# A graph network's node update: the last tile's product made while edges are counted, and six half groups instead of ten between a layer's steps

## The reference

```python
x_norm = layer_norm(x, norm_g, norm_b)
out1 = gat_conv(x_norm, src, dst, W1, a_src1, a_dst1, b1, 4, 192, N)   # "layer A"
out2 = gat_conv(out1, src, dst, W2, a_src2, a_dst2, b2, 2, 96, N)      # "layer B"
x = _layernorm(x + (concatenate([x, out2], -1) @ Wu + bu))
x = _layernorm(x + second_block(x, ...))                               # "layers C and D"
```

## Time and profile before

| | us |
|---|---|
| median of 3 runs (1874.57 to 1877.85) | 1876.23 |
| the profiled execution's own time | 1875.85 |
| its span, first to last instruction | 1874.0 |
| PE busy, DVE busy, ACT busy | 1775.2, 1540.3, 744.5 |
| counting of edges, the windows' products on PE | 18.9 to 256.4 |
| layer B's steps on PE | 549.6 to 612.0 |

### The profile page before, as it was taken

One profiled execution on the slowest core, in us unless ns is written; L12 is line 12 of the kernel. 1 busy time (PEld: TensorE's weight loads), 2 busy tenths in 40 slices (PEclk: granted clock), 3 DMA queues, 4 the chain that ended last, 5 costly groups with the idle time before them and its releaser, 6 DMA issues.

```text
span 1874.0 us, 24445 instructions
## 1 busy us (share of the span) xinstructions
PE 1775.2 (95%) x8514; PEld 1337.5 (71%) x8515; DVE 1540.3 (82%) x2913; ACT 744.5 (40%) x1279; POOL 21.9 (1%) x40
## 2 busy tenths in 40 slices
PE   6799977799999999999999999998999989999997
PEld 3544545799654655555999999997999965555554
DVE  7889979999569538999999999996467458998996
ACT  5899979534134221111444444443211222332331
POOL 0000011010000000000000000000000000000000
PEclk8989989899999999999999999998999999999999
DMA  6200159541440447676222221210466567767764
GB/s 187 69 19 27 60 203 388 162 120 31 144 146 12 173 148 251 216 239 188 90 70 75 60 86 58 88 30 30 137 191 208 167 228 255 247 222 250 249 218 162
DMA packets 168068, 276.67 MB, mean 148 GB/s; under 512 B 11819, under 2 KB 132386, under 8 KB 164486
## 3 DMA queue, kind: packets, MB, share of 16 engines
q1 hardware_dynamic: 115942, 212.43, 34.7%
q10 hardware_dynamic: 48736, 48.48, 8.0%
q0 software_dynamic: 3264, 14.16, 2.0%
HBM read 219.31 MB, written 55.71 MB: 147 GB/s over the span
## 4 chain that ended last, share of the span: by engine, by line
PE 83%; DVE 8%; ACT 4%; DMA 3%; issue 2%; ACTq 0%; DVEq 0%; SPq 0%
PE ps L1432 26%; PE ps L1461 17%; PE ps L1379 12%; PE ps L1283 10%; PE ps L1077 4%; PE ps L1094 4%; PE ps L1186 2%; PE ps L1215 2%; PE ps L1334 1%; DVE work L2463 1%; ACT work L1548 1%; DVE work L2457 1%; ACT work L1625 1%; DVE feat L2120 1%; DVE feat L2428 1%
## 5 line engine op out<-in xcount | busy, mean ns | idle before, releaser
L1461 PE MATMUL ps<-work 128*128 128x384 f32 (+1 forms) x784 | 256.7, 486 | 2.4 <-DVE work L2213 2.4
L1432 PE MATMUL ps<-counts,work 128*128 128x193 f32 x1440 | 239.3, 327 | 0.0
L1379 PE MATMUL ps<-work 128*128 128x384 f32 (+1 forms) x720 | 236.4, 489 | 0.0
L1432 PEld LDWEIGHTS ps<-counts,work 128*128 128x128 f32 x1440 | 235.9, 190 | 0.3 <-DVE work L2463 0.3
L1863 ACT ACTIVATE work<-work,s 128x1280 f32<-128x1280 f32 x111 | 151.4, 1364 | 212.0 <-DVE work L2457 210.3
L1461 PEld LDWEIGHTS ps<-work 128*128 128x128 f32 x784 | 148.4, 189 | 107.8 <-DVE work L2213 3.6
L1379 PEld LDWEIGHTS ps<-work 128*128 128x128 f32 x720 | 136.4, 190 | 96.5 <-issue 15.9
L2463 DVE SCALAR_TENSOR_TENSOR work<-work,counts 128x1280 f32<-128x1280 f32 x112 | 166.4, 1486 | 0.1
L2028 DVE TENSOR_SCALAR work<-work,winoff 125x480 bf16<-125x480 f16 x480 | 158.1, 397 | 5.0 <-PE ps L1094 4.8
L1432 PE MATMUL ps<-counts 128*128 128x193 f32 x960 | 160.9, 327 | 1.1 <-ACTq L574 1.1
L1432 PEld LDWEIGHTS ps<-counts 128*128 128x128 f32 x960 | 157.4, 190 | 1.8 <-ACTq L574 1.8
(11 more groups left out here) (301 smaller groups left out, 2602.7 us busy)
## 6 DMA issues: line engine op xcount, KB each, us to landing
work<-hs_d SPq DMA_DIRECT2D x75, 960.0 KB, 5.3
work<-nomask_d SPq DMA_DIRECT2D x70, 320.0 KB, 3.3
work<-pqrow_d SPq DMA_DIRECT2D x12, 1280.0 KB, 6.4
nomask_d<-work SPq DMA_DIRECT2D x40, 320.0 KB, 7.8
hx_d<-work ACTq DMA_DIRECT2D x60, 192.0 KB, 2.7
counts<-hx_d SPq DMA_DIRECT2D x120, 96.0 KB, 1.9
hs_d<-feat ACTq DMA_DIRECT2D x22, 480.0 KB, 3.7
counts<-pqrow_d SPq DMA_DIRECT2D x6, 1280.0 KB, 6.2
```

The source lines that it names most:

```text
L1379: last = mm(bank(n % 4 if i else n % 2, cols), xT[:, j, t * P:(t + 1) * P], wv[:, j, :], start=(j == 0), stop=(j == DT - 1))
L1432: last = mm(sums_at(c, t, u), xe_of(c)[i % RING][:, t * P:(t + 1) * P], hx[:, i % RING, 0:1 + c.width], start=(r == 0 and k == 0 and t % T ...
L1461: last = mm(bank(product_bank(g, i), width), a[:, at * P:(at + 1) * P], h_block(n, block_, width), start=(m == 0), stop=(m == STEPS_D - 1) ...
```

## The change

The last tile's product (two groups) leaves layer B and is made among the windows of the count, behind windows 23 and 25 (`U_LAST_AT`), from `xT`, which lies in SBUF there. For it:

- SP loads both halves of Wu's upper part once more (2 DMAs of 1152 KB), into the still free `TOTAL` part of `counts`, behind its last load of `xT`.
- GpSimd adds the identity to them (six additions more, `own_part`).
- PE gets two groups of six products (`u_last_half`), the first behind a wait for `u_diag`, the second behind ACT's copy of the first, since both use PSUM bank 7.
- ACT gets two copies and one DMA (`u_last_fetch`), and DVE's first `total_counts` (behind window 33) waits until that DMA has landed.
- `ALL_LO` ends at window 22 instead of 26: in windows 23 to 26 ACT makes four source rows instead of six, and DVE two.
- In layer B 18 groups are left. Groups 0 to 14 stand where they stood; three groups, six half groups, stand behind steps 0, 3, 6, 9, 12 and 15 instead of ten behind 0, 2, ..., 16 and 17.

```diff
-ALL_LO = range(17, 27)
+ALL_LO = range(17, 23)
...
-U_GROUPS = 2 * T
+U_GROUPS = 2 * (T - 1)
+U_LAST_AT = (23, 25)
...
-U_AFTER_STEP = {i: (U_BEFORE + n // 2, n % 2) for n, i in enumerate([0, 2, 4, 6, 8, 10, 12, 14, 16, 17])}
+U_AFTER_STEP = {i: (U_BEFORE + n // 2, n % 2) for n, i in enumerate([0, 3, 6, 9, 12, 15])}
...
+            sp.wait_ge(m_done, 2 * DT)
+            for q in range(2):
+                sp.dma_start(wu_early[q], t_in["Wu"][0:D, q * 384:(q + 1) * 384].rearrange("(j p) c -> p j c", p=P)) \
+                    .then_inc(u_in, 16)
...
+            pool.wait_ge(u_in, 16 * 2)
+            own_part(wu_early)
...
+            def u_last_half(q):
+
+                if q == 0:
+                    pe.wait_ge(u_diag, 1)
+                    pe.wait_ge(xt_a_in, 16 * DT)
+                    pe.wait_ge(xt_a_zero, 1)
+                    pe.wait_ge(crow_saved, 1)
+                else:
+                    pe.wait_ge(u_ev, 1)
+                for j in range(DT):
+                    last = mm(bank(7, 384), xT[:, j, (T - 1) * P:T * P], wu_early[q][:, j, :], start=(j == 0), stop=(j == DT - 1))
+                last.then_inc(u_mm, 1)
...
+                    if w in U_LAST_AT:
+                        u_last_half(U_LAST_AT.index(w))
...
+            def u_last_fetch(q):
+                act.wait_ge(u_mm, q + 1)
+                nc.scalar.activation(u_last[:, q * 384:(q + 1) * 384], bank(7, 384), ACT.Copy).then_inc(u_ev, 1)
+                if q:
+                    act.wait_ge(u_ev, 2)
+                    act.dma_start(base_d[(T - 1) * P:T * P, :], u_last).then_inc(u_out[0], 16)
...
+                dve.wait_ge(*u_left(T - 1))
```

More of the change, by code:

```diff
@@ L251, in gnn_program @@
         wt_a = flat_f[TOTAL][0:96, 0:8 * D]
+        wu_early = [flat_f[TOTAL][:, q * DT * 384:(q + 1) * DT * 384].rearrange("p (j c) -> p j c", j=DT) for q in range(2)]
+        u_last = flat_f[TOTAL][:, 2 * DT * 384:2 * DT * 384 + D]
         wg = [carve(feat, 0, DT * A_COLS[0]).rearrange("p (j c) -> p j c", j=DT),
@@ L609, in rows_bank, with u_left @@
             return 0 if c is B else 5
+        def u_left(t):
+            return (u_out[0], 16) if t == T - 1 else (u_out[t % 3], 16 * (t // 3 + 1 + (t % 3 == 0)))
         def u_bank(g):
@@ L787, in layer, with base_left @@
                                 .then_inc(s.pq_in[h].sem, 16)
-                        sp.wait_ge(u_mm, U_GROUPS)
+                        sp.wait_ge(u_mm, U_LAST + U_GROUPS)
+                        def base_left(t):
+                            sp.wait_ge(*u_left(t))
                         for t in BASE_FIRST:
-                            sp.wait_ge(u_out[t % 3], 16 * (t // 3 + 1))
+                            base_left(t)
                             base_load(t)
                         for t in BASE_LAST:
-                            sp.wait_ge(u_out[t % 3], 16 * (t // 3 + 1))
+                            base_left(t)
                         end_phase(sp, ph)
@@ L932, in _, with own_part @@
             nc.gpsimd.memset(xT[:, :, N:NP], 0.0).then_inc(xt_a_zero, 1)
+            def own_part(wu):
+                for j in range(DT):
+                    w_ = wu[j // 3][:, j, j % 3 * P:(j % 3 + 1) * P]
+                    last = nc.gpsimd.tensor_tensor(w_, w_, identf[:, :], ALU.add)
+                last.then_inc(u_diag, 1)
+            pool.wait_ge(u_in, 16 * 2)
+            own_part(wu_early)
             pool.wait_ge(*sems[A].proj_mm.at(2 * T))
@@ L941, in _ @@
             end_phase(pool, 0)
-            pool.wait_ge(u_in, 16 * 2)
-            for j in range(DT):
-                w_ = wu_half[j // 3][:, j, j % 3 * P:(j % 3 + 1) * P]
-                last = nc.gpsimd.tensor_tensor(w_, w_, identf[:, :], ALU.add)
-            last.then_inc(u_diag, 1)
+            pool.wait_ge(u_in, 16 * 4)
+            own_part(wu_half)
             end_phase(pool, 1)
@@ L1058, in turn_a_rows @@
                         pe.wait_ge(crow_saved, 1)
+                        pe.wait_ge(u_ev, 2)
                     o = 3 * 512 + t * P if t < 8 else 7 * 512 + (t - 8) * P
@@ L1119, in _ @@
                     m_unit(i)
+                for q in range(2):
+                    u_last_half(q)
                 for n in range(2 * T):
@@ L1198, in bias_product @@
                     pe.wait_ge(wub_in, 16 * 4)
-                    pe.wait_ge(u_ev, U_EARLY)
+                    pe.wait_ge(u_ev, U_LAST + U_EARLY)
                 else:
@@ L1467, in _ @@
             layer(0, A, 0)
-            pe.wait_ge(u_diag, 1)
+            pe.wait_ge(u_diag, 2)
             pe.wait_ge(*sems[A].saved.at(5 * T))
@@ L1579, in _ @@
                         g_unit(n)
+                    if w - 1 in U_LAST_AT:
+                        u_last_fetch(U_LAST_AT.index(w - 1))
             with act.Else():
@@ L1592, in _ @@
                     m_unit(i)
+                for q in range(2):
+                    u_last_fetch(q)
                 deviations()
@@ L1778, in u_fetch @@
                         if q == 0 and t >= 3:
-                            act.wait_ge(u_out[t % 3], 16 * (t // 3))
-                        act.wait_ge(u_mm, g + 1)
+                            act.wait_ge(*u_left(t - 3))
+                        act.wait_ge(u_mm, U_LAST + g + 1)
                         nc.scalar.activation(u_stage[t % 3][:, q * 384:(q + 1) * 384], bank(u_bank(g), 384), ACT.Copy) \
```

7 lines of the change are left out of this document (4 added, 3 removed).

## The result

The changed kernel took 1882.02 us (median of 20 runs, 1876.54 to 1887.32) and the kernel before 1878.68 us beside it (20 runs, 1873.97 to 1883.42): a ratio of 1.0025, 95% interval 1.0016 to 1.0033. The medians lie 3.3 us apart; the ratio says 4.7 us (3.0 to 6.2), and where this text has one number for the loss it is that one. The forecast was 1878.4 us and "no change that can be told". The profiled execution took 1880.85 us, its span 1878.9 us.

The account below looks back on a forecast made before the run. PE, busy 95% of the span, was taken as the bound where it is waited for. 1875.85 + 3.3 (count) - 1.1 (layer B) = 1878.05 us profiled, 1878.4 as the median; range 1873.5 to 1883.

Parts of the forecast that it names:

- The count, +3.3 us: Count from window 22 on: two groups add 7.8 us on PE, partly regained; net +3.3, bounds +1.7 and +6.9.
- 4.3 us come back from the gaps and from the earlier clock: Count, windows 22 to 28: of 7.8 us added, closed PE gaps and an earlier clock rise return 4.3.
- Layer B, -1.1 us: Layer B's steps: four half groups fewer end the phase at 613.0 instead of 614.1 us; bounds -0.5 and -1.7.
- DVE's wait: Layer B's steps: each half group stops DVE for 1.0 us, once in three steps.
- the period: Layer B's steps: three steps take 9.58 us, against 9.36 us before the change.
- the handovers: Layer B's steps: two handovers between engines, estimated at 0.2 us each, with 0.1 and 0.3 as bounds.
- the phase ends with PE or ACT: End of layer B: PE's transposes or ACT's copy end the phase at 613.0 us, no longer a store.
- The change touches two places: Whole kernel: the change acts only in the count (+3.3 us) and in layer B's steps (-1.1 us).
- The first (half groups vanish): Layer B's steps: half groups cost DVE nothing in PE's gaps, phase 6.6 us earlier, net -3.3, 1872.9 us; chance 0.10.
- the second: Count, first added group: PE waits for GpSimd's additions at 3.3 us each; net +8.7, 1884.9 us; chance 0.10.
- the third: Count: PE's clock doesn't rise before projection 0; net +5.8, 1882.0 us; chance 0.14.
- the fourth: Count: the added groups hide wholly in PE's earlier waits, costing 0; net -1.1, 1875.1 us; chance 0.08.

Follow-up runs that it names:

- e8: Kernel before with only `ALL_LO` ending at window 22 instead of 26; 1872.19 us, ratio 0.9977, and 1873.44 us, ratio 0.9977, in a second comparison.
- e5: Changed kernel with masks' units, last tile's product and groups of g left out of PE's never-taken branch of the count; 1879.29 us, ratio 1.0017 to the kernel before.
- e10: Changed kernel with only the last tile's product left out of PE's never-taken branch, making it as long as before; 1881.88 us, ratio 1.0021 to the kernel before.
- e2: Changed kernel with layer B's 20 groups and ten half groups as before, so the last tile is made twice; 1887.89 us (5 runs), ratio 1.006 to the kernel before.
- e3: Kernel before with 24 matmuls added in PE's never-taken branch of the count; 1880.9 us against 1877.9, ratio 1.0017.
- e4: Changed kernel with GpSimd's first weight loads held back until PE has turned two masks; 1887.01 us, ratio 1.0055 to the kernel before.

## Why the prediction was wrong

1. *The count, +3.3 us.* Right in mechanism and nearly in size. From window 22 on the three profiles of the changed kernel take 166.0 us each and those of the kernel before 162.1 in the mean: +3.8. Over the nine profiles with this order on PE it is 164.5 to 166.2 us, +3.4 in the mean, the shorter the sooner the clock rose. Unbroken run, rise of the clock, both groups and the place of every window came as written. e8 splits the term, which the prediction had as one: the shares of the one-hots give 3.7 us, and the added groups cost 7.6 us (166.0 against 158.4; 6.1 to 7.8 over the nine), nearly all of their 7.8. The sentence "4.3 us come back from the gaps and from the earlier clock" was right as a sum, but that gain didn't need the groups.
2. *Layer B, -1.1 us.* Measured -1.6, near the bound of -1.7; the term was under-sized by 0.5. DVE's wait is 0.84 us and not 1.0, the period 9.52 and not 9.58, which is 0.3 us over five periods. Two errors nearly cancel in the period: the handovers are 0.03 and 0.04 us and not 0.2 each, but the step behind PE's wait takes 2.39 us and not 2.15. That the phase ends with PE or ACT held.
3. *The failed step* is the first sentence on the change: "The change touches two places". It touches a third, through its code. Twelve products and their waits, in each of two branches, move the masks' code. Two blocks of instructions instead of one then have to land before PE can start the first mask, which makes it 1.7 us later behind DVE's mask, and PE stands once more, 4.0 to 4.8 us, in the second mask: +3.5 us (93.1 against 89.6 in the means of three profiles each), with no term in the sum and no rival for it. 3.8 - 1.6 + 3.5 = +5.7 by stages. The profiled spans differ by 4.0 in the mean, the chance of the clock and of attention A (0.9 and 0.6 us in favour of the changed kernel) being most of the rest; the ratio says 4.7 and the medians 3.3.
4. *The rivals.* The first (half groups vanish), the second (GpSimd: 0.45 us an addition where it decides from 2.7), the third (the clock) and the fourth didn't happen. Against the second the prediction named idle times of DVE of 2.5 us and more from 82 to 99 us; there is one of 2.52 and one of 0.79. The chances were formed from them alone, and so 0.69 lay on no change. The side that came had 0.24, for reasons that were wrong.
5. *The time itself*, 1882.0, lies in the range of 1873.5 to 1883.0, but only as the range had room for the third rival. A part of the distance is the base: the kernel before took 1876.23 us in the three runs that the sum starts from and 1878.68 in the 20 beside the change.

A rule that would have raised the question was to be had. The Trainium skill (Runtime: NRT & Kernel Launch, Instruction fetch mechanics) says that engines get instructions in 16 KiB blocks that are prefetched in sequence, and that a taken branch to code outside the loaded blocks must wait for its block. The trace agrees on the size (1.16 MB in 71 packets of the instruction queue) and on the stall; the jump over the branch stands right ahead of the masks. Here the first block kept PE up to 7.1 us, of which the wait for DVE's mask (4.1 us in e5) would have hidden most, and a second 1.3 to 4.8 us. That the kernel before waits for a block at the same jump could have been seen beforehand, in the 0.70 us between DVE's mask and PE's start. The rule gives no argument by length, though: e10 shows that.

What stays open: which instruction lies at which block's border, which no view shows; most of e2's 11 us; and what moves the masks' stage by up to 5 us behind the sixteenth mask (e8).

## What to carry to other kernels

When a change adds or removes instructions around a branch, look behind the jump for waits that nothing releases, for a late start behind the releaser that the profile names, and for blocks in the instruction queue, and give the sum a term for it; here it was 3.5 us, and code that never runs could bring it about (e3). Try each number of a compound change by itself: here one line, `ALL_LO`, gave 3.7 us against 1.6 from layer B, and what it was meant to make room for cost twice as much. And where a difference of 2 us is to be explained, take three profiles of each kernel before explaining anything, and look first at the granted clock behind each wait of PE.

## What was not expected of the hardware

- 24 products that are never executed made the kernel 0.17% slower [1.0002, 1.0031], with a wait of 3.83 us at a mask.
- In the changed kernel PE stood 6.6 to 7.1 us at the first mask, with the bulk loads beside it or (e4) held back.
- An addition of 128x128 f32 on GpSimd took 0.44 to 0.53 us, whether DVE stood idle or made one-hots, where the earlier trace rows had 2.03 us beside DVE's two-input steps.
- The same program starts its window 22 at 91.4 or at 94.9 us, and its attention A takes 138.8 or 141.0 us. In the executions that are slower in attention A the granted clock is 0.50 for a stretch behind a wait of PE.
